# Another assignment of images and channels to the 128 partitions, in a kernel that moves its rows by indirect DMA

## The reference

```
x -> _gn(x)         32 groups of 12 channels: (g - mean) / sqrt(var + 1e-5)
  -> _displace      xg[b, pos, ch, y - oy, x - ox], 0 outside
  -> conv 3x3       kern = exp(-(dx*dx + dy*dy) / (2 * 0.5**2)), normalised, one for each position
return x + that
```

## Time and profile before

| what | value |
|---|---|
| time, median of 3 | 976.11 us |
| the profiled execution's own time | 978.52 us |
| its span (first to last instruction) | 976.7 us |
| DVE busy | 871.0 us (89%) |
| ACT busy | 714.3 us (73%) |
| POOL busy | 326.6 us (33%) |
| PE busy | 201.4 us (21%) |
| DMA, queue of POOL | 402.67 MB, 99.0% of 16 engines' span |
| mean rate of all DMA over the span | 413 GB/s |

### The profile page before, as it was taken

The page is one execution under the profiler, slowest core; times in us unless marked ns, Lnnn a source line. Parts: engine busy times, 40 slices in busy tenths (PEclk is TensorE's granted clock), DMA queues, the critical chain, the costliest instruction groups (busy, mean ns, idle before and its releaser), DMA issues.

```text
span 976.7 us, 3636 instructions
## 1 busy us (share of the span) xinstructions
PE 201.4 (21%) x896; PEld 195.9 (20%) x896; DVE 871.0 (89%) x940; ACT 714.3 (73%) x412; POOL 326.6 (33%) x196
## 2 busy tenths in 40 slices
PE   0331312212122121222202212212122122220120
PEld 0331312212122121222202212212122122220120
DVE  5389899999999999799999999999999979679990
ACT  3998959777687686878777786868778787878720
POOL 3032352443514333142315263252522423224320
DMA  8999999999999999999999999999999999999996
GB/s 358 428 368 421 420 422 414 424 404 395 415 426 411 405 423 412 424 421 429 429 424 419 417 415 416 421 407 429 418 419 419 417 428 427 422 431 406 428 429 280
DMA packets 28233, 403.48 MB, mean 413 GB/s; under 512 B 3506, under 2 KB 3506, under 8 KB 3634
## 3 DMA queue, kind: packets, MB, share of 16 engines
q0 software_dynamic: 27648, 402.67, 99.0%
q1 hardware_dynamic: 562, 0.57, 0.2%
HBM read 201.90 MB, written 201.33 MB: 413 GB/s over the span
## 4 chain that ended last, share of the span: by engine, by line
DVE 48%; DMA 39%; issue 5%; ACT 4%; POOL 3%; POOLq 0%; ACTq 0%; DVEq 0%
DMA out<-tiles,row_of 30%; DVE tiles L437 17%; DVE rowblur L412 8%; DMA tiles<-x,row_of 8%; DVE tiles L439 8%; DVE rowblur L417 8%; DVE normed L396 5%; POOL tiles L187 3%; ACT unread L242 3%; ACT unread L246 1%; DVE scale L351 0%; DVE shift L354 0%; DVE var_p L341 0%; DVE apart L335 0%; DVE apart L337 0%
## 5 line engine op out<-in xcount | busy, mean ns | idle before, releaser
L242 ACT ACTIVATE unread<-tiles 128x4096 uint8<-128x4096 f32 x94 | 339.9, 3616 | 167.6 <-DMA tiles<-x,row_of 167.0
L246 ACT ACTIVATE unread<-tiles,nmean_p 128x4096 uint8<-128x4096 f32 x94 | 348.7, 3709 | 3.0
L187 POOL DMA_INDIRECT tiles<-x,row_of x96 | 156.8, 1633 | 518.0 <-DMA out<-tiles,row_of 512.6
L437 DVE SCALAR_TENSOR_TENSOR tiles<-rowblur,ratio,tiles 128x735 f32<-128x735 f32 (+24 forms) x192 | 300.0, 1562 | 4.6
L216 PE MATMUL mean_ps<-nmean_p,mask 128*128 128x1 f32 x448 | 100.7, 353 | 562.7 <-ACT unread L242 535.3
L216 PEld LDWEIGHTS mean_ps<-nmean_p,mask 128*128 128x128 f32 x448 | 98.0, 330 | 565.3 <-ACT unread L242 538.0
L192 POOL DMA_INDIRECT out<-tiles,row_of x96 | 169.7, 1768 | 109.6 <-DVE tiles L437 85.3
L412 DVE SCALAR_TENSOR_TENSOR rowblur<-normed,ratio 128x784 f32<-128x784 f32 (+14 forms) x96 | 152.2, 1586 | 3.4
L439 DVE TENSOR_TENSOR tiles<-rowblur,tiles 128x784 f32<-128x784 f32 (+14 forms) x96 | 146.5, 1526 | 3.3
L417 DVE SCALAR_TENSOR_TENSOR rowblur<-normed,ratio,rowblur 128x752 f32<-128x752 f32 (+14 forms) x96 | 145.5, 1515 | 3.4
L216 PE MATMUL var_ps<-var_p,mask 128*128 128x1 f32 x448 | 100.7, 354 | 174.6 <-DVE var_p L341 174.6
(11 more groups left out here) (34 smaller groups left out, 25.7 us busy)
## 6 DMA issues: line engine op xcount, KB each, us to landing
tiles<-x,row_of POOLq DMA_INDIRECT x96, 14.9
out<-tiles,row_of POOLq DMA_INDIRECT x96, 17.6
mask<-masks SPq DMA_DIRECT2D x1, 448.0 KB, 3.2
row_of<-rows SPq DMA_DIRECT2D x1, 48.0 KB, 1.8
offs<-offset SPq DMA_DIRECT2D x1, 48.0 KB
plan_sb<-planned SPq DMA_DIRECT2D x1, 0.4 KB
offs_p<-offset SPq DMA_DIRECT2D x1, 0.4 KB
steps_sb<-steps SPq DMA_DIRECT2D x1, 12.0 KB
```

The source lines that it names most:

```text
L187: pool.indirect_dma_start(tiles[:, n % SLOTS, :], None, x_rows, bass.IndirectOffsetOnAxis(ap=row_of[:, n:n + 1], axis=0)).then_inc(loaded[ ...
L242: nc.scalar.activation(unread[:], tiles[:, n % SLOTS, :], ACT.Identity, scale=-1.0 / HW, accum_out=nmean_p[:, i % 2, j:j + 1]).then_inc(nm ...
L246: nc.scalar.activation(unread[:], tiles[:, n % SLOTS, :], ACT.Square, bias=nmean_p[:, i % 2, j:j + 1], accum_out=m2_p[:, i % 2, j:j + 1]). ...
L437: ins = nc.vector.scalar_tensor_tensor(y, t, ratio[:, (tap + 1) // 2, p, 1:2], y, ALU.mult, ALU.add)
```

## The change

The image and the channel that a partition holds come from another formula. Before, the channel was p div 4 mod 8, and the image 2 * (p div 32 mod 2 * 4 + p mod 4) + p div 64. Now the image is p mod 16, and the channel p div 16. The table of rows and the masks are made from the same two arrays, so they follow.

```diff
 def image_of_partition():
 
     p = np.arange(128)
-    return 2 * (p // 32 % 2 * 4 + p % 4) + p // 64, p // 4 % CH
+    return p % BT, p // BT
```

## The result

The changed kernel takes 980.76 us (median of 20 executions, 975.85 to 986.96), the kernel before 975.28 us (median of 20, 968.89 to 982.02). The ratio is 1.0062, with a 95% interval of 1.0043 to 1.0081. The change costs about 6 us. The interval lies wholly above 1, so the kernel is slower, but within the 1% that the prediction called no change, and at a fifth of the 28 us that it forecast.

A forecast was written before the change was run, and what follows sets the result against it. The prediction took POOL's full DMA queue as the bound, DVE second. Instructions 0, bytes 0 and slower packets + 28 us on a 976.1 us median gave about 1004 us; likeliest case 986 to 1035, 8 in 10 between 960 and 1090.

The forecast's parts named there:

- What bounds the kernel: Whole kernel: POOL's DMA queue, 99.0% full, bounds it, DVE second; a longer packet lengthens it almost one for one.
- Instructions and bytes: All engines and the queue: same instructions, waits, operand shapes, packets and bytes; DVE, ACT, PE, POOL times stand; cost 0.
- Direction: Rows moving at the same moment: two images abreast become four, 24 MiB apart; packets get slower; chance of slower 0.58.
- How far the DMA is from its best: Body, 25 to 951 us: 418 GB/s against 431 in the best stretch, a loss of 28 us through longer packets.
- The stretch 12 to 50 us: First loads, only reads, at 429 GB/s; taken to show that neighbouring rows alone are no trouble.
- The term itself: Slower packets in the body: today's loss of 28 us doubles, + 28 us, body rate about 406 GB/s.
- No change: Rival, chance 0.32: engines drift apart, so any formula gives a mixture abreast; 418 GB/s again, 970 to 985 us.
- Much slower: Rival, chance 0.20: rows a large power of two apart meet in the same part of memory; 1035 to 1300 us.
- Its estimate of 1010 us: Under the much slower rival: time scaled by the Trainium skill's 207 GB/s for 512 KiB row distance, against 214 full rate.
- Faster: Rival, chance 0.10: today's slow spells come from eight neighbours abreast and go when spread; 28 us less at most, 948 us.

The follow-up runs named there:

- c_sbuf: Formula of before, computation left out; a store waits for six tap-like DVE operations in their own SBUF area: 970.7 us, 0.9908 of the full kernel before.
- c_dve: Formula of before, transfers with DVE's normalise and taps only; ACT's passes, PE and statistics left out: 970.3 us, 0.9927 of the full kernel before.
- e9_sp_piece: Full kernel, but SP issues direct transfers of 128 adjacent rows instead of POOL's indirect ones: 956.3 us, 0.9798 of the kernel before.
- c_free: Formula of before, computation left out; DVE works unpaused in its own SBUF area, stores wait for loads only: 972.0 us, 0.9924 of the full kernel before.

## Why the prediction was wrong in size

**What bounds the kernel: right.** The queue's share is 98.8%, before 99.0%. A longer packet lengthened the kernel nearly one for one: 6.9 us of excess to 8.4 us of time between the two profiled executions.

**Instructions and bytes: right, but for POOL in the profile.** Packets, bytes and the busy times of DVE, ACT and PE are unchanged. POOL's 327 us became 337: the issue of a load takes 1738 ns instead of 1633. POOL waits 517 us for stores, so this did not bound the kernel.

**Direction: right.** The arrangement of rows was all that was left to cost anything, and it did cost.

**"How far the DMA is from its best": the step that failed.** It priced the loss against the best stretch at 28 us, rightly, but then let all of it stand for the memory. "The losses of today show that the memory side does get in the way when some rows meet" was the sentence. The transfers alone have 4.8 us of excess, not 26.7. The rest appears only with the computation, about two thirds of it with DVE at work in SBUF (c_sbuf and c_dve, 15 us of 22). The computation takes the same toll under the formulas of before and after (0.0225 and 0.0221 of the ratio). Doubling 28 us therefore doubled a loss that the change doesn't touch. The stretch 12 to 50 us in the earlier trace rows held a hint: 429 GB/s, with DVE busy for 17.55 us of 38 and POOL issuing next to nothing. I read it as evidence on neighbouring rows alone.

**The term itself.** + 28 us was forecast, + 5.5 us measured by the medians (6 by the ratio). The doubling was a choice without a measurement and can't be rescued by a smaller base either: alone, the excess went from 4.8 to 20.6 us in the profiled executions, four times, and the time by 8.7 us in the medians. In the full kernel about 6 us remain.

**The rivals.** "No change", within 1%, is where the time came to lie, though not for its reason: the rows don't mix so far that the formula is irrelevant, as 1.0193, 1.0182 and 1.1163 show. Nor is 1% the least that can be told from no change, as the prediction has it; with 20 executions of each the interval is 0.4% wide. "Much slower" has a real mechanism, 11.6% at 8 MiB, but the changed formula is far from it. (Its estimate of 1010 us comes out at 1009 when worked out again.) "Faster" is refuted with its premise: the neighbours are not the cause, since sixteen adjacent rows are the fastest arrangement.

**What stays open.** Why four images at 6 MiB cost 1.8% and at 24 MiB 0.6%, which rows of neighbouring turns meet, and by what way DVE makes packets longer while further transfers are queued. The loss of about 15 us to DVE's work in SBUF is shown, but for the question of the second array; that it goes through POOL's descriptors is supported by e9_sp_piece and not settled. About 7 us of what the computation costs have no cause found. No kernel that computes the reference was faster than the one before.

## What to carry to other kernels

When a DMA queue is full and its rate is still some per cent under its best, ask first what the loss depends on, before any of it is charged to the suspect of the day: the transfers alone, with everything else taken out, cost one run and split it. Which row goes to which partition is a knob worth a per cent or two with no instruction changed; here, neighbouring rows in the sixteen partitions were the cheapest (0.991), and rows 8 MiB apart by far the dearest (1.116). Between the two, measure: four images cost 0.6% or 1.8% by their arrangement, and nothing here foretells which. A chain of waits that swings from 48% DVE to 74% DMA over 0.6% of time says only that both are nearly full.

## What the runs showed of the hardware

- A 16 KB packet takes 611 ns on its engine at the median, in the kernels before and after and with the transfers alone. That is 26.8 GB/s, or 429 GB/s for sixteen; the best slices show 431 to 433.
- POOL's issue of a 128-row indirect load takes 975 ns alone, the same beside ACT's passes (972) or beside DVE in PSUM (975), and 1656 to 1674 ns beside DVE in SBUF (c_dve, c_sbuf and c_free). For a store it is 955 to 958 ns and 1752 to 1817.
- Beside DVE's work in SBUF the transfers took 970.3, 970.7 and 972.0 us, against 954.6 us alone; beside its work in PSUM 955.6 us, and beside ACT's passes 956.2 us.
- Rows 8 MiB apart in the sixteen partitions (4 MiB in the last 32 tiles) make the transfers alone 12.5% longer than the formula of before (1074.3 against 954.6 us); sixteen images at 6 MiB make the full kernel 1.9% longer, and sixteen adjacent rows 0.9% shorter.
- A direct transfer of 16 x 8 rows from SP ran at half rate in the first loads (203 to 215 GB/s, in an execution of 1342 us), while one of 128 adjacent rows ran at 427 to 433 over most of the kernel.
